# Adding the two output tensors of a four-block layer stack: through SBUF and VectorE, or as accumulating DRAM to DRAM transfers

## The reference

```
pos = position of the token among those of its expert
dispatch = zeros(64, 64, 256).at[expert, pos].set(x, mode='drop')
y = silu(dispatch @ w_gate.T) * (dispatch @ w_up.T) @ w_down.T
out[token] = sum over its 8 experts of weight * y[expert, pos]   (dropped ones count nothing)
```

## Time and profile before

| | us |
|---|---|
| median of 3 runs | 4304.78 (4302.63 to 4305.23) |
| profiled execution, its own time | 4291.18 |
| profiled execution, span from the first to the last instruction | 4289.1 |
| TensorE busy in the span | 3884.6 (91%) |
| VectorE busy | 3610.1 (84%) |
| ScalarE busy | 2635.9 (61%) |
| GpSimd busy | 2219.0 (52%) |
| last stage, from the end of the meeting before it to the end of the span | 4250.12 to 4289.1 |

### The profile page before, as it was taken

One profiled execution on the slowest core, in us unless ns is written; L12 is line 12 of the kernel. 1 busy time (PEld: TensorE's weight loads), 2 busy tenths in 40 slices (PEclk: granted clock), 3 DMA queues, 4 the chain that ended last, 5 costly groups with the idle time before them and its releaser, 6 DMA issues. The chain is left out here.

```text
span 4289.1 us, 54983 instructions
## 1 busy us (share of the span) xinstructions
PE 3884.6 (91%) x17786; PEld 2959.5 (69%) x17786; DVE 3610.1 (84%) x4517; ACT 2635.9 (61%) x3523; POOL 2219.0 (52%) x1837
## 2 busy tenths in 40 slices
PE   7959978759999999999999999999999999989563
PEld 4635536538888888888888888888888888867321
DVE  7845549859999999999999999999999999946511
ACT  6624334337777777777777777777777777732221
POOL 2547757825555555555555555555555555520164
PEclk9969989969999999999999999999999999989776
DMA  7224447842233222332223322223222232056286
GB/s 270 55 53 65 67 118 247 283 85 56 50 69 67 56 56 50 66 71 55 57 50 63 75 52 61 51 61 76 52 59 51 57 79 52 15 160 220 86 240 163
DMA packets 335313, 388.12 MB, mean 90 GB/s; under 512 B 141516, under 2 KB 263185, under 8 KB 322483
## 3 DMA queue, kind: packets, MB, share of 16 engines
q1 hardware_dynamic: 310966, 358.28, 32.7%
q0 software_dynamic: 24064, 26.32, 3.6%
HBM read 236.66 MB, written 117.79 MB: 83 GB/s over the span
## 5 line engine op out<-in xcount | busy, mean ns | idle before, releaser
L1561 POOL TENSOR_TENSOR at_pl<-at_pf,at_ph 128x512 fp32r<-128x512 f32 x1024 | 1330.6, 1299 | 1341.1 <-ACT at_ph L1708 1340.8
L1707 ACT ACTIVATE at_pf<-at_ps_s 128x1024 f32<-128x1024 f32 x1024 | 1051.2, 1027 | 745.7 <-PE at_ps_s L1757 745.7
L1624 DVE TENSOR_TENSOR at_pl<-at_pf,at_ph 128x512 fp32r<-128x512 f32 x1024 | 1355.4, 1324 | 20.6 <-ACT at_ph L1708 20.6
L1606 DVE TENSOR_REDUCE at_mx<-at_ps_u 128x2 f32<-128x1024 f32 x1024 | 1249.8, 1220 | 22.5 <-PE at_ps_u L1741 22.4
L1708 ACT ACTIVATE at_ph<-at_ps_s 128x1024 fp32r<-128x1024 f32 x1024 | 1043.1, 1019 | 0.0
L1757 PE MATMUL at_ps_s<-at_q,at_k 66*128 66x512 f32 x2048 | 819.7, 400 | 0.0
L1756 PE MATMUL at_ps_s<-at_q,at_k 128*128 128x512 f32 x2048 | 811.4, 396 | 0.5 <-ACT at_ph L1708 0.5
L1773 PE MATMUL at_ps_v<-at_ph,at_vh 128*128 128x512 f32 x2048 | 809.2, 395 | 0.2 <-POOL at_pl L1561 0.2
L1775 PE MATMUL at_ps_v<-at_pl,at_vh 128*128 128x512 f32 x2048 | 809.1, 395 | 0.0
L1774 PE MATMUL at_ps_v<-at_ph,at_vl 128*128 128x512 f32 x2048 | 808.1, 395 | 0.0
L1741 PE MATMUL at_ps_u<-at_k,at_qp 128*128 128x512 f32 x2048 | 647.5, 397 | 64.2 <-DMA at_q<-at_low 48.4
(11 more groups left out here) (261 smaller groups left out, 4034.2 us busy)
## 6 DMA issues: line engine op xcount, KB each, us to landing
at_k<-kT SPq DMA_DIRECT2D x64, 512.0 KB, 10.1
at_q<-qT SPq DMA_DIRECT2D x64, 512.0 KB, 9.2
wgu<-Wgu_in SPq DMA_DIRECT2D x64, 384.0 KB, 5.2
qT<-pj_rot SPq DMA_DIRECT2D x32, 512.0 KB, 5.2
vT<-pj_vo SPq DMA_DIRECT2D x16, 1024.0 KB, 5.7
kT<-pj_rot SPq DMA_DIRECT2D x32, 512.0 KB, 3.2
at_raw<-qT SPq DMA_DIRECT2D x32, 512.0 KB, 4.8
at_raw<-kT SPq DMA_DIRECT2D x32, 512.0 KB, 6.7
```

The source lines that it names most:

```text
L1561: pool.tensor_tensor(pl[:, n % NP, at], pf[:, n % NP, at], ph[:, n % NP, at].bitcast(F32), ALU.subtract).then_inc(s["pl2_ready"], 1)
L1606: dve.tensor_reduce(mx[:, qb % 2, 2 * i:2 * i + 2], ps_u[:], X, ALU.max).then_inc(s["u_max"], 1)
L1624: dve.tensor_tensor(pl[:, n % NP, at], pf[:, n % NP, at], ph[:, n % NP, at].bitcast(F32), ALU.subtract)\
L1707: act.activation(pf[:, n % NP], ps_s[:, n % 2], ACT.Exp, scale=DH ** -0.5)
```

## The change

The four loads from either tensor, VectorE's additions and the stores go, and so do the two buffers in SBUF. In their place GpSimd issues four transfers, each of 1024 rows (1 MB) from `out_odd` to the same rows of `out`, both in DRAM, which add what they read to what is there. `max_dma_last_dim=8192` caps a contiguous piece of a transfer at 8192 bytes, that is 2048 numbers; rows that follow each other in both tensors make one contiguous run. At the end GpSimd waits for all four.

```diff
         with ctx:
-            even = sb("even", [P, NT, D])
-            odd = sb("odd", [P, NT, D])
-            s = {n: sem(n) for n in "in0 in1 in2 in3 added stored".split()}
+            s = {n: sem(n) for n in ["stored"]}
             block = ctx.enter_context(nc.Block())
 
-            def part(q, of=None):
-                tiles = slice(q * NT // QUARTERS, (q + 1) * NT // QUARTERS)
-                return tiles if of is None else of.rearrange("(n p) d -> p n d", p=P)[:, tiles]
-
-            @block.sync
-            def _(sp):
+            @block.gpsimd
+            def _(pool):
                 for q in range(QUARTERS):
-                    sp.dma_start(even[:, part(q)], part(q, self.out)).then_inc(s[f"in{q}"], 16)
-                    sp.dma_start(odd[:, part(q)], part(q, self.out_odd[:])).then_inc(s[f"in{q}"], 16)
-                for q in range(QUARTERS):
-                    sp.wait_ge(s["added"], q + 1)
-                    sp.dma_start(part(q, self.out), even[:, part(q)]).then_inc(s["stored"], 16)
-                sp.wait_ge(s["stored"], 16 * QUARTERS)
-
-            @block.vector
-            def _(dve):
-                for q in range(QUARTERS):
-                    dve.wait_ge(s[f"in{q}"], 32)
-                    dve.tensor_tensor(even[:, part(q)], even[:, part(q)], odd[:, part(q)], ALU.add)\
-                        .then_inc(s["added"], 1)
+                    rows = slice(q * T // QUARTERS, (q + 1) * T // QUARTERS)
+                    pool.dma_start(self.out[rows], self.out_odd[rows], accum_op=ALU.add, max_dma_last_dim=8192).then_inc(s["stored"], 16)
+                pool.wait_ge(s["stored"], 16 * QUARTERS)
```

## The result

The changed kernel takes 4289.87 us in the median of 7 runs, against 4305.23 us in the median of 7 runs of the kernel before: a ratio of 0.9964, with a 95% interval from 0.9953 to 0.9975, that is 10.8 to 20.2 us. Forecast were 4291.5 us and a gain of 13.3.

What follows compares the result with a forecast made beforehand. The prediction took DMA throughput to bound the last stage, 38.98 us. New terms 0.05 + 1.77 + 0.54 + 21.1 + 2.2 = 25.7 us, a gain of 13.3, so 4304.78 − 13.3 = 4291.5 us; range 4284 to 4312.

Steps and rivals of the forecast that it cites:

- (a): Last stage: GpSimd's first transfer issue takes 1.77 us; the other three issues lie under the first transfers.
- (b): Last stage: from the end of the issue to the first moving byte, 0.54 us.
- (c): Last stage's accumulating transfers: each 8 KB piece costs two reads plus 31 ns, 659 ns; 21.1 us in all; chance 0.48.
- (d): Last stage: from the last byte to the end of the span, kept at 2.2 us.
- The stage is bound by DMA throughput: Last stage before the change, 38.98 us: full DMA engines set its time, not VectorE's additions of 2.29 us each.
- The constant of 31 ns: Accumulating transfers: cost of a piece beyond its two reads, 135 less 104 ns for 1 KB rows.
- DRAM is the limit: Rival for the transfers: DRAM's 12.58 MB can't pass 417 GB/s, so 30.2 us, result 4300.6; chance 0.17.
- The addition costs by the byte: Rival for the transfers: 116 ns per 256 numbers added, larger pieces save nothing; 29.7 us, result 4300.1; chance 0.12.
- Pieces don't overlap: Slower rival for the transfers: each piece holds its engine until written; 51.7 us, result 4322.1; chance 0.12.
- Cheaper than two reads: Rival for the transfers: the second read is hidden; 11.0 us, result 4281.4; chance 0.06.
- Pieces stay 1 KB: Rival for the last stage: the change doesn't enlarge pieces; stage 44.1 us, result 4309.9; chance 0.05.
- the meeting before the stage stays as it is: Before the last stage: the meeting of all engines is unchanged, as GpSimd is already the last to arrive.

## Why the prediction was right

Term by term, in the chain of the profiled execution: from the end of the meeting to the first issue 0.51 us (0.05 forecast); (a) the issue 0.93 (1.77); (b) to the first byte, at 4266.65, 0.7 (0.54); (c) the transfers to 4286.4, 19.8 (21.1); (d) the end 3.0 (2.2). The sum is 24.9 us against a forecast of 25.7, and the saving of the stage 14.1 us against 13.3. From the scatter it is 13.9, because the meeting took 0.1 us longer (10.15 us from the issue's end to its own end, against 10.02). The measured 15.4 us have an interval that holds all of these. That the sum is off by under 1 us is in part luck: (a) and (c) were forecast 2.1 us too long together, the other terms 1.4 us too short.

- *The stage is bound by DMA throughput* was right, and what it rests on is now shown by an edit: larger pieces alone, with VectorE's work left as it was, shorten it.
- *(c), two reads a piece*, agrees with every run and is within 7% in size. Three things bear on it: from SBUF the pace stays (214 and 213 GB/s), 213 is half of the 425 GB/s at which 8 KB pieces load, and the pace over three sizes has twice the slope of loads. The constant of 31 ns was mis-sized, since it was taken from bursts of 4 and 8 rows an engine. In steady flow all that is left beside the bytes is 8 ns a piece. The prediction's own rows gave 116 ns for each further row, 12 ns over two reads; with 12 in place of 31, (c) would have been 20.5 us.
- *DRAM is the limit* (0.17): refuted for the addition, by 639 GB/s in all where 417 was the supposed cap, and by the run from SBUF. It stays open for the plain copy, whose 77 ns over a load no run here explains.
- *The addition costs by the byte* (0.12): its price, 116 ns a KB, isn't there; even at 1 KB the pace is 84 ns. That the adding itself takes the time of one further read can't be told from the second read, as no run adds without reading twice. So the price of two reads is shown, and the reading of the destination as its cause is argued.
- *Pieces don't overlap* (0.12) was wrong: at 1 KB, where it would hurt most, packets overlap by almost a quarter.
- *Cheaper than two reads* (0.06): 11.0 us of transfers were its price, and 19.8 were measured.
- *Pieces stay 1 KB* (0.05): they didn't, 512 of 8 KB. The price that the prediction gave to this case was wrong, 44.1 us for the stage where a kernel with 1 KB pieces took 27.4 (the 26.9 of the table and the 0.5 before the first issue). Both its terms, 6.7 us an issue and 34.6 us of transfers, had been drawn from indirect scatters: 5.5 ns a piece of GpSimd's time there, 0.5 here. With it, the case would have been faster, not within the noise.
- By the Trainium skill (Collectives: The Full Stack, section on the bandwidth ceiling and the fold count), with a copy at 31 GB/s an engine and half of it for a reduce, the estimate for (c) was 16.9 us. The runs gave 19.8, and a plain copy at 334 / 16 = 20.9 GB/s an engine.

The runs with moved waits show what the prediction left out. It said that the meeting before the stage stays as it is, and that was so; but the 10 us there were read as a fixed price, and 4.8 us of the time from the scatter can be had (36.5 to 31.7).

## What to carry to other kernels

A stage that only adds one DRAM tensor to another was here a stage of passes through the DMA engines: count what each form reads and writes per byte, at the rate of its piece size, and an accumulating transfer counts as two reads. A form that needs no buffer can also be moved into the stage before; but look at what stands behind the last byte before and after the move, and try an engine other than GpSimd for the last wait, which was worth 4.4 us here. A price taken from short indirect transfers overstated a long direct one.

## What the runs showed of the hardware that was not expected

- Accumulating transfers from DRAM to DRAM write 196, 210 and 211 to 215 GB/s with pieces of 1, 4 and 8 KB; the piece size matters less than for plain loads, which go from 348 to 425 GB/s.
- GpSimd issues a direct transfer of 128 pieces in 0.93 us, of 512 in 1.13 and of 1024 in 1.40, where an indirect one of 128 rows took up to 1.81 us.
- The total of DRAM bytes that the page gives counts an accumulating transfer's source and not the destination that it reads: the page of the changed kernel has 4.19 MB less read than that of before (236.66 MB), though both read both tensors, and just as much as that of the plain copy, which reads one.

```profile
HBM read 232.47 MB, written 117.79 MB: 82 GB/s over the span
```

- The way out of a stage is not a fixed price: after the last bytes 3.0 us in the small stage, 6.5 to 6.6 in the stage of the pairs with SyncE, ScalarE or TensorE as the last, and 10.8 with GpSimd.
